# A hybrid attention kernel in one core: another order of its one list of steps

## The chip, the cores and the metric

One NeuronCore of a Trainium2 chip runs the kernel. The metric is the device time of one execution in microseconds. An engine of the core works through its own list of instructions in order and waits on semaphores for the others: PE (TensorE, the matmuls), ACT (ScalarE), DVE (VectorE), POOL (GpSimd), and SP, which here only issues transfers. An instruction that waits holds up everything behind it on its engine.

## What is computed

`x` holds 8 batches of 1024 tokens with 256 channels. The reference, cut to its core:

```
x = x + conv(gn(x))            # group norm; qkv = x @ w_qkv; q and k layer-normed per head;
                               # dots = k^T v per head; out = q @ dots / 1024
t = x + attn(ln(x))            # 8 heads of 32: softmax(q k^T / sqrt(32)) v, then @ w_agg + b_agg
t = t + ffn(ln(t))             # gates = 8 rounds of Sinkhorn; each of 8 experts takes its
                               # 128 best tokens per batch, multiplies by its 256 x 256 weights
```

## The kernel before

**Three things at a time.** While the softmax attention of batch b runs, the kernel does the linear attention and the projections of batch b+1 (the "front" steps) and the aggregation and layer norm of batch b-1 (the "store" steps). So the program is: a prologue with the front of batch 0 alone; eight stretches, one per batch attended, called batch 0 to batch 7 here; and a tail with the last store and the expert part. Batches 1 to 6 have all three kinds of work. Batch 0 has no store, batch 7 no front. Sinkhorn rounds are merged into batch 6, the selection of tokens into batch 7.

**Slots.** The attention of a batch is 64 units: scores of 128 keys by 256 queries by 4 heads on PE (L829, 4 matmuls), an exponential on ACT (L1123), the weighing by v on PE (L851). Eight units make a block, whose sum of probabilities DVE adds up (L1489, units 1 to 6 of a block). Two units are a slot, so that a batch has 32 slots, and a block ends every fourth slot: PE sums (`total`, L861), ACT copies the accumulator (L1113), DVE inverts it (L1474), POOL divides (L1156).

**The list of steps.** Everything else is a step. `order()` (L85) gives one hand-written list, in which `("rest", n)` leaves n slots empty; `spread()` (L70) deals the list to slots by the costs in `WORK`, and every engine walks the same plan. In a slot PE issues the scores of the next slot's two units, the first half of the steps, the weighing of its own two units, the second half. ACT has one exponential ahead of each half. DVE adds up between the halves. POOL has the steps only, and a division at the start of every slot with k % 4 = 1.

**The steps named below.** `xT` (c, h): 4 transposes of x on PE (L868), a copy on ACT (L1051), statistics on DVE. `agg` (t): aggregation on PE (L873), added and measured on DVE (L1255, L1249). `store_stats` and `head_stats`: chains of small POOL instructions for a reciprocal square root, each waiting for the one before. `store_rows` (t): the normalised rows on ACT (L1030). `z2T` and `gate`: transposes and gate logits of stored tokens. `gmean`, `gvar`, `xn`: the group norm of x. `qk0`, `v0`: queries, keys and values of the linear attention. `resid` (t): POOL adds the bias (L1192). `head_scale` (quarter): two instructions (L743); quarters 0 to 2 on POOL and 3 on DVE in batches 0 to 6. `qT` (c, h): transposes of scaled queries; h = 1 needs all four quarters. `dots`: 32 matmuls `shared<-rows,lo`. `lin` (t): its result times the queries. `zT`, `proj`, `v`, `norms`: the projections for the next attention. PE steps share two PSUM banks in turn: a step may start once the step two before it has been read.

## Time and profile before

| | |
|---|---|
| median of 3 runs | 1663.41 us (1662.82 to 1664.5) |
| profiled execution | 1661.75 us, span 1659.0 us |
| PE busy | 1390.6 us, 84% of the span |
| DVE busy | 1061.8 us, 64% |
| ACT busy | 872.8 us, 53% |
| POOL busy | 587.9 us, 35% |
| mean granted TensorE clock | 0.922 |

The prologue ends at 122.4 us, batch 0 runs to 279.6, batches 1 to 6 to 1315.5, batch 7 to 1454.6, and the rest is the tail. PE is the busiest engine in all of it but the tail. A granted clock of 1.00 is 2.4 GHz and 0.50 is 1.2 GHz.

### The profile page before, as it was taken

What the parts mean: (1) busy time and instruction counts of PE and PEld (TensorE: products, weight loads), DVE (VectorE), ACT (ScalarE), POOL (GpSimd) and SP (SyncE); (2) the same over time, 40 slices, a digit from 0 to 9 for tenths busy, and PEclk for the clock granted to TensorE, in tenths of its full rate; (3) what the DMA queues carried; (4) which work ended last, traced back from release to release, by engine and by line L of the source; (5) the groups of instructions that cost most, each with busy time, mean ns of one, the idle gap of its engine ahead of it and who ended that gap; (6) DMA issues with size and microseconds to landing.
All of it is one profiled execution on the core that took longest, in us unless ns stands there. A gap on an engine that the chain in (4) does not pass through costs nothing.

```text
span 1659.0 us, 27948 instructions
## 1 busy us (share of the span) xinstructions
PE 1390.6 (84%) x10311; PEld 923.7 (56%) x10311; DVE 1061.8 (64%) x2037; ACT 872.8 (53%) x1251; POOL 587.9 (35%) x1142
## 2 busy tenths in 40 slices
PE   5678899898989898989898999899988978976553
PEld 3445556556656656665656565656554655555432
DVE  3326776767675767585848585767678798645721
ACT  2336666666666566656665766566655555521100
POOL 1401520553034404341444134412442032455664
PEclk8889999999989999999999999999999988878777
DMA  2033004400440035003500260027000550243442
GB/s 70 26 91 75 1 26 106 125 13 26 92 138 13 27 77 153 13 27 72 158 14 6 68 182 14 1 58 197 14 2 1 117 166 11 83 148 112 128 144 71
DMA packets 66014, 119.07 MB, mean 72 GB/s; under 512 B 10321, under 2 KB 46162, under 8 KB 65874
## 3 DMA queue, kind: packets, MB, share of 16 engines
q1 hardware_dynamic: 56640, 92.04, 20.7%
q0 software_dynamic: 8192, 25.17, 4.9%
q8 instruction: 85, 1.39, 0.3%
q14 instruction: 55, 0.45, 0.1%
q10 hardware_dynamic: 1042, 0.01, 0.0%
HBM read 29.11 MB, written 33.55 MB: 38 GB/s over the span
## 4 chain that ended last, share of the span: by engine, by line
PE 51%; DVE 20%; issue 9%; POOL 8%; ACT 7%; SPq 2%; another core or an unknown queue 2%; DMA 0%; ACTq 0%; POOLq 0%; DVEq 0%
PE shared L873 29%; PE acc L851 8%; PE scores L829 8%; DVE prob_sum L1489 7%; PE shared L868 3%; DVE acc_sb L1474 3%; ACT probs L1123 2%; PE acc L861 2%; PE acc L848 1%; POOL out_dram L1228 1%; DVE bn L1249 1%; DVE best_i L1406 1%; POOL lo L743 1%; DVE work L1408 1%
## 5 line engine op out<-in xcount | busy, mean ns | idle before, releaser
L1123 ACT ACTIVATE probs<-scores 128x1024 f32<-128x1024 f32 x512 | 515.2, 1023 | 271.1 <-DVE prob_sum L1489 136.1
L1489 DVE TENSOR_TENSOR prob_sum<-prob_sum,probs 128x512 f32<-128x512 f32 x640 | 423.9, 722 | 0.0
L829 PE MATMUL scores<-query_stack,key_stack 96*128 96x256 f32 x2048 | 344.8, 308 | 44.7 <-ACT probs L1123 41.0
L829 PEld LDWEIGHTS scores<-query_stack,key_stack 96*128 96x128 f32 x2048 | 279.1, 196 | 123.2 <-ACT probs L1123 77.3
L851 PE MATMUL acc<-probs,v_all 128*32 128x256 f32 x4096 | 302.1, 402 | 0.4 <-issue 0.4
L1156 POOL TENSOR_TENSOR attn_T<-acc_sb 128x256 f32<-128x256 f32 x64 | 54.9, 858 | 546.8 <-DVE acc_sb L1474 537.0
L873 PE MATMUL shared<-w_sb,chan 128*128 128x512 f32 (+1 forms) x512 | 186.3, 500 | 5.0 <-DVE chan L1310 5.0
L851 PEld LDWEIGHTS acc<-probs,v_all 128*32 128x32 f32 x4096 | 117.2, 113 | 116.2 <-issue 43.8
L873 PE MATMUL shared<-chan,w1T 128*128 128x512 f32 x256 | 127.3, 622 | 8.8 <-DVE lo L1359 6.4
L1489 DVE TENSOR_TENSOR prob_sum<-probs 128x512 f32<-128x512 f32 x128 | 92.4, 762 | 56.6 <-PE acc L861 49.6
L873 PEld LDWEIGHTS shared<-w_sb,chan 128*128 128x128 f32 x512 | 91.1, 191 | 62.3 <-issue 56.0
L1474 DVE RECIPROCAL acc_sb<-acc_sb 128x256 f32<-128x256 f32 x64 | 111.6, 1744 | 21.9 <-ACT acc_sb L1113 21.1
L1359 DVE TENSOR_TENSOR lo<-shared,hi 128x512 fp32r<-128x512 f32 x64 | 44.1, 689 | 98.5 <-ACT hi L1076 98.5
L873 PE MATMUL shared<-lo,hi 128*128 128x256 f32 x256 | 77.3, 456 | 34.3 <-DVE chan L1444 17.4
L1325 DVE TENSOR_REDUCE ss<-v_all 128x16 f32<-128x512 f32 x64 | 43.6, 682 | 83.4 <-ACT v_all L1065 82.9
L1058 ACT ACTIVATE lo<-shared 128x512 f32<-128x512 f32 x64 | 38.2, 597 | 97.9 <-PE shared L873 97.9
L1106 ACT ACTIVATE hi<-shared 128x512 f32<-128x512 f32 x32 | 19.1, 597 | 134.2 <-remote 47.0
L873 PE MATMUL shared<-waggT,attn_T 128*128 128x256 f32 x256 | 74.2, 432 | 15.1 <-DVE resid L1255 14.8
L873 PEld LDWEIGHTS shared<-lo,hi 128*128 128x128 f32 x256 | 55.9, 229 | 48.0 <-DVE chan L1444 18.5
L1076 ACT ACTIVATE hi<-shared 128x512 fp32r<-128x512 f32 x64 | 38.2, 598 | 75.4 <-PE shared L873 75.4
L873 PEld LDWEIGHTS shared<-chan,w1T 128*128 128x128 f32 x256 | 45.3, 195 | 56.9 <-issue 42.8
L868 PE MATMUL shared<-ident,rows 128*128 128x128 f32 x256 | 47.2, 299 | 33.1 <-ACT rows L1030 23.2
(168 smaller groups left out, 2016.5 us busy)
## 6 DMA issues: line engine op xcount, KB each, us to landing
query_stack<-hi SPq DMA_DIRECT2D x128, 128.0 KB, 2.5
key_stack<-hi SPq DMA_DIRECT2D x128, 128.0 KB, 2.5
x_sb<-in_x_dram SPq DMA_DIRECT2D x8, 1024.0 KB, 5.6
key_stack<-lo SPq DMA_DIRECT2D x64, 128.0 KB, 2.5
query_stack<-lo SPq DMA_DIRECT2D x64, 128.0 KB, 2.4
out_dram<-resid SPq DMA_DIRECT2D x16, 512.0 KB
tokens_scratch<-resid SPq DMA_DIRECT2D x16, 512.0 KB
tokens_scratch<-rows SPq DMA_DIRECT2D x16, 512.0 KB, 3.3
```

Of the source, the lines that this page charges most:

```text
L829: last = pe.matmul(score_ps[u % 2][:, QB * r:QB * (r + 1)], key_stack[stack, HG * g + r, P * kt:P * (kt + 1)], query_stack[stack, HG * g + ...
L851: last = pe.matmul(acc[DH * r:DH * (r + 1), 0:QB], v_all[:, g, kt, DH * r:DH * (r + 1)], p[:, QB * r:QB * (r + 1)], start=kt == 0, stop=kt ...
L868: last = pe.transpose(ps[:, P * j:P * (j + 1)], m, ident[:, :])
L873: last = pe.matmul(out, stationary, moving, start=j == 0, stop=j == len(pairs) - 1)
L1058: read(act.activation(qk0[:, at[0], :], ps[:, :], ACT.Copy), seg, *st)
L1076: act.activation(hi[:, j, BANK * h:BANK * (h + 1)].bitcast(F32R), ps[:, :], ACT.Copy) \
L1123: act.activation(probs[:, u % PROBS, :], score_ps[u % 2][:, :], ACT.Exp, scale=DH ** -0.5) \
L1156: pool.tensor_tensor(attn_T[:, g, QB * qb:QB * (qb + 1)], acc_sb[:, 0:QB], acc_sb[:, QB:2 * QB], ALU.mult).then_inc(s["attn_ready"], 1)
L1325: dve.tensor_reduce(ss[:, t, :], squares[:, t % 2, :].rearrange("p (h d) -> p h d", d=DH), AX.X, ALU.add).then_inc(s["squares_summed"], 1)
L1359: read(dve.tensor_tensor(lo[:, j, part].bitcast(F32R), ps[:, :], hi[:, j, part], ALU.subtract), seg, *st)
L1474: dve.reciprocal(acc_sb[:, QB:2 * QB], acc_sb[:, QB:2 * QB]).then_inc(s["recip_ready"], 1)
L1489: dve.tensor_tensor(total[:, part], probs[:, (u - 1) % PROBS, part] if kt == 1 else total[:, part], probs[:, u % PROBS, part], ALU.add).th ...
```

## The change

Only the list in `order()` changes. Every step of before is still there once, in another place; `WORK`, `spread()` and the engines' code are the same. `rest` entries move, and shorter ones are used. Since the same plan also sets which PSUM bank a step gets, the turns of the two banks change with it.

```diff
-    steps = [("agg", 0), ("agg", 1), ("agg", 2), ("agg", 3), ("xT", 0, 0), ("xT", 0, 1), ("rest", 0.5),
+    steps = [("xT", 1, 0), ("xT", 0, 1), ("agg", 0), ("rest", 0.5), ("agg", 1), ("agg", 2), ("agg", 3),
...
-             ("head_scale", 1), ("head_stats", 1), ("rest", 1), ("resid", 6), ("resid", 7), ("sumv",), ("qT", 0, 0),
+             ("resid", 5), ("v0", 7), ("head_scale", 1), ("head_stats", 1), ("rest", 1), ("head_scale", 2),
```

Dealt to slots, batches 1 to 5 read so at the places of interest (a bar between the halves of a slot):

```
slot   before                                          after
0      agg0 agg1 agg2 | agg3 xT00 xT01                 xT10 xT01 | agg0 agg1
1      store_stats0 xT10 | agg4 xT11                   agg2 agg3 store_stats0 | xT11 xT00 agg4
2      agg5 x_stats agg6 gmean agg7 |                  agg5 x_stats agg6 store_rows0 gmean |
         store_rows0 gvar store_rows1 store_stats1       gvar agg7 store_rows1 store_stats1 store_rows2
3      z2T0 store_rows2 z2T1 | store_rows3 z2T2        z2T0 z2T1 | store_rows3
4      z2T3 | gate0                                    z2T2 z2T3 | xn0 gate0
5      xn0 | xn1
6                                                      qk00 gate1 | store_rows4
7      qk00 |                                          xn1 |
8      store_rows4 gate1 z2T4 v00 store_rows5 |        store_rows5 gate2 z2T4 store_rows6 |
         qk01 gate2 store_rows6 gate3                    gate3 v00 qk01 z2T5
12     resid4 v06 qk07 head_scale0 |                   resid4 v06 qk07 head_scale0 |
         resid5 v07 head_scale1                          resid5 v07 head_scale1 head_stats1
13     head_stats1 |
14     resid6 resid7 sumv | qT00 qT10 head_scale2      head_scale2 qT10 | qT00
15                                                     resid6 | sumv
16     head_scale3 |                                   head_scale3 | resid7
17     qT01 qT11 | dots                                qT11 | dots
19     lin0 | lin1                                     lin0 qT01 | lin1 lin2
20     lin2 lin3 front_stats0 | lin4 lin5 lin6         lin3 lin4 | front_stats0
21     lin7 |                                          lin5 lin6 | lin7
23     front_rows3 |                                   front_rows3 | zT10
24     zT00 zT10 | proj00                              zT00 front_rows4 front_rows5 | proj00 proj10
27-31  the same
```

First place: PE at the start of batch 1, slots 0 and 1. `waggT,attn_T` is agg (two matmuls each), `x_sb` is xT (four each). Before:

```order
L829 MATMUL scores<-query_stack,key_stack 128x256 x8
L873 MATMUL shared<-waggT,attn_T 128x256 x6
L861 MATMUL acc<-prob_sum,ones 32x256 x4
L851 MATMUL acc<-probs,v_all 32x256 x8
L873 MATMUL shared<-waggT,attn_T 128x256 x2
L868 MATMUL shared<-ident,x_sb 128x128 x8
L829 MATMUL scores<-query_stack,key_stack 128x256 x8
L868 MATMUL shared<-ident,x_sb 128x128 x4
L851 MATMUL acc<-probs,v_all 32x256 x8
L873 MATMUL shared<-waggT,attn_T 128x256 x2
L868 MATMUL shared<-ident,x_sb 128x128 x4
L829 MATMUL scores<-query_stack,key_stack 128x256 x8
```

And after:

```order
L829 MATMUL scores<-query_stack,key_stack 128x256 x8
L868 MATMUL shared<-ident,x_sb 128x128 x8
L861 MATMUL acc<-prob_sum,ones 32x256 x4
L851 MATMUL acc<-probs,v_all 32x256 x8
L873 MATMUL shared<-waggT,attn_T 128x256 x4
L829 MATMUL scores<-query_stack,key_stack 128x256 x8
L873 MATMUL shared<-waggT,attn_T 128x256 x4
L851 MATMUL acc<-probs,v_all 32x256 x8
L868 MATMUL shared<-ident,x_sb 128x128 x8
L873 MATMUL shared<-waggT,attn_T 128x256 x2
L829 MATMUL scores<-query_stack,key_stack 128x256 x8
```

Two xT now stand ahead of the first agg and the first `total`, and agg 0 to 3 fall on both sides of the scores of slot 1.

Second place: POOL in batch 1, from quarter 1 of head_scale (the first L743) to the start of the second head_stats chain (L336, then L338). L1156 is the division of a block. Before:

```order
L743 TENSOR_TENSOR lo<-lo,hr 128x512 x2
L1192 TENSOR_TENSOR resid<-lin_out,bias 128x256
L743 TENSOR_TENSOR lo<-lo,hr 128x512 x2
L1156 TENSOR_TENSOR attn_T<-acc_sb 128x256
L336 TENSOR_SCALAR hr<-ss 128x64
L338 TENSOR_TENSOR hh<-hr 128x64
```

After:

```order
L743 TENSOR_TENSOR lo<-lo,hr 128x512 x2
L1192 TENSOR_TENSOR resid<-lin_out,bias 128x256
L743 TENSOR_TENSOR lo<-lo,hr 128x512 x2
L336 TENSOR_SCALAR hr<-ss 128x64
L338 TENSOR_TENSOR hh<-hr 128x64
```

The division has left its place ahead of the chain. What follows the chain on POOL, from its third-last instruction on, before:

```order
L339 TENSOR_TENSOR hh<-hh,ss 128x64
L340 TENSOR_SCALAR hh<-hh 128x64
L341 TENSOR_TENSOR hr<-hr,hh 128x64
L1192 TENSOR_TENSOR resid<-lin_out,bias 128x256 x2
L743 TENSOR_TENSOR lo<-lo,hr 128x512 x2
L1156 TENSOR_TENSOR attn_T<-acc_sb 128x256
```

And after:

```order
L339 TENSOR_TENSOR hh<-hh,ss 128x64
L340 TENSOR_SCALAR hh<-hh 128x64
L341 TENSOR_TENSOR hr<-hr,hh 128x64
L1156 TENSOR_TENSOR attn_T<-acc_sb 128x256
L743 TENSOR_TENSOR lo<-lo,hr 128x512 x2
L1192 TENSOR_TENSOR resid<-lin_out,bias 128x256 x2
L1156 TENSOR_TENSOR attn_T<-acc_sb 128x256
```

The division comes behind the chain, and the two resid have gone from ahead of head_scale 2 to behind it.

Third place: PE in batch 1, slots 6 to 8. `w_sb,chan 128x512` is qk0, `w_sb,chan 128x256` is v0, `gate_w,hi` is gate, `ident,rows` is z2T. Before:

```order
L829 MATMUL scores<-query_stack,key_stack 128x256 x8
L873 MATMUL shared<-w_sb,chan 128x512 x2
L851 MATMUL acc<-probs,v_all 32x256 x4
L848 MATMUL acc<-probs,ones 32x256 x4
L851 MATMUL acc<-probs,v_all 32x256 x4
L829 MATMUL scores<-query_stack,key_stack 128x256 x8
L873 MATMUL shared<-gate_w,hi 128x8 x2
L868 MATMUL shared<-ident,rows 128x128 x2
L873 MATMUL shared<-w_sb,chan 128x256 x2
```

And after:

```order
L829 MATMUL scores<-query_stack,key_stack 128x256 x8
L873 MATMUL shared<-w_sb,chan 128x512 x2
L873 MATMUL shared<-gate_w,hi 128x8 x2
L851 MATMUL acc<-probs,v_all 32x256 x8
L829 MATMUL scores<-query_stack,key_stack 128x256 x8
L851 MATMUL acc<-probs,v_all 32x256 x4
L848 MATMUL acc<-probs,ones 32x256 x4
L851 MATMUL acc<-probs,v_all 32x256 x4
L829 MATMUL scores<-query_stack,key_stack 128x256 x8
L873 MATMUL shared<-gate_w,hi 128x8 x2
L868 MATMUL shared<-ident,rows 128x128 x2
```

qk0 0 and gate 1 come in slot 6, one slot and two slots earlier, and slot 7 has no PE step of its own.

## Rows read from the trace of the kernel before

**Rows 1.** Stretches of batch 3: length, busy us of engines, granted clock, DMA.

```profile
core 0: us, PE busy (x) PEld busy (x) DVE busy (x) ACT busy (x) POOL busy (x), PEclk, DMA share, GB/s
622.70:651.10 28.40, 24.97 (x212) 18.02 (x208) 20.48 (x52) 16.29 (x25) 9.40 (x31) 0.94 0.81 223
651.10:661.40 10.30, 9.10 (x86) 5.30 (x86) 9.80 (x17) 6.52 (x8) 9.31 (x13) 1.00 0.01 2
661.40:699.50 38.10, 35.75 (x245) 22.96 (x241) 17.46 (x34) 24.03 (x42) 15.08 (x29) 1.00 0.04 15
699.50:725.20 25.70, 21.38 (x190) 15.44 (x189) 19.06 (x24) 13.88 (x17) 14.10 (x19) 0.87 0.00 1
725.20:747.60 22.40, 19.21 (x207) 13.67 (x205) 20.24 (x45) 14.00 (x18) 8.21 (x24) 1.00 0.15 49
747.60:793.00 45.40, 43.95 (x308) 26.74 (x308) 27.97 (x42) 31.07 (x47) 3.40 (x12) 1.00 0.31 70
```

**Rows 2.** Chain that ended last, batches 3 and 4: start, us, what.

```profile
711.67 2.32 POOL resid L1192 x2
713.99 2.92 POOL lo L743 x2
...
882.01 2.32 POOL resid L1192 x2
```

**Rows 3.** Timeline of PE, batch 3: start, us, what, idle before and releaser.

```profile
637.31 3.64 PE L873 MATMUL shared<-waggT,attn_T 128*128 128x256 f32 x8 [2.23 <-DVE resid L1255]
...
663.84 0.41 PE L868 MATMUL shared<-ident,rows 128*128 128x128 f32 x2 [0.87 <-ACT rows L1030]
...
717.00 1.94 PE L868 MATMUL shared<-ident,lo 128*128 128x128 f32 x8 [3.66 <-POOL lo L743]
...
720.73 4.71 PE L873 MATMUL shared<-rows,lo 128*128 128x128 f32 x32
```

**Rows 4.** Granted clock in short stretches, columns as in rows 1.

```profile
637.30:640.70 3.40, 3.39 (x8) 2.55 (x9) 1.66 (x6) 1.24 (x2) 2.00 (x10) 0.50 0.91 231
717.00:722.60 5.60, 5.60 (x32) 4.00 (x33) 3.53 (x5) 2.60 (x4) 1.05 (x1) 0.50 0.00 1
```

**Rows 5.** Timeline of DVE, batch 3, slots 0 to 2.

```profile
631.51 1.74 DVE L1474 RECIPROCAL acc_sb<-acc_sb 128x256 f32<-128x256 f32 x1
...
634.44 2.48 DVE L1489 TENSOR_TENSOR prob_sum<-prob_sum,probs 128x512 f32<-128x512 f32 x4
636.84 0.41 DVE L1255 TENSOR_TENSOR resid<-shared,resid 128x256 f32<-128x256 f32 x1
```

**Rows 6.** Timeline of POOL, batch 3: store_stats 1, then head_stats 1.

```profile
650.97 0.44 POOL L1167 TENSOR_SCALAR ln_v<-mv 128x4 f32<-128x4 f32 x1 [0.20 <-POOL small L341]
...
653.67 2.77 POOL L340 TENSOR_SCALAR ln_h<-ln_h 128x4 f32<-128x4 f32 x1
...
656.98 3.99 POOL L338 TENSOR_TENSOR ln_h<-ln_r 128x4 f32<-128x4 f32 x1
...
662.17 0.23 POOL L1161 TENSOR_SCALAR ln_b<-ln_b 128x4 f32<-128x4 f32 x1
...
702.59 1.15 POOL L1156 TENSOR_TENSOR attn_T<-acc_sb 128x256 f32<-128x256 f32 x1 [4.18 <-DVE acc_sb L1474]
703.82 0.57 POOL L336 TENSOR_SCALAR hr<-ss 128x64 int32<-128x64 int32 x1
```

**Rows 7.** Timeline of DVE, batch 3, slots 4 to 7 and slot 12.

```profile
653.07 0.91 DVE L1310 TENSOR_SCALAR chan<-chan,small 128x512 f32<-128x512 f32 x2
653.89 2.49 DVE L1489 TENSOR_TENSOR prob_sum<-prob_sum,probs 128x512 f32<-128x512 f32 x4
...
699.49 0.67 DVE L1325 TENSOR_REDUCE ss<-v_all 128x16 f32<-128x512 f32 x1
```

**Rows 8.** Timeline of PE, batch 0: its dots, and a wait ahead of them.

```profile
198.00 1.22 PE L829 MATMUL scores<-query_stack,key_stack 96*128 96x256 f32 x4 [1.80 <-ACT probs L1123]
...
206.20 3.84 PE L873 MATMUL shared<-rows,lo 128*128 128x128 f32 x32
```

40 lines of the change are left out of this document (20 added, 20 removed).

## The prediction

> **What bounds the kernel now.** I read the stretches of one batch first, then the chain, then PE's timeline at its waits, and last the timeline of the engine that each wait names. Batches 1 to 6 are 1036 of the 1659 us and repeat themselves: the two resid of batches 3 and 4 start at 711.67 and 882.01, a period of 170.34 us [rows 2]. So I work on batch 3 and multiply by six. In its six stretches PE is busy 154.36 of 170.3 us, while DVE has 115.0 and ACT 105.8 [rows 1]. PE is the bound, and only two things can be had from it without taking work away: its idle time, 15.9 us, and the time in which its clock is at 0.50. Both sit at few places. The first stretch (slots 0 to 4) has 3.43 us idle, slots 5 to 7 have 1.20, slots 8 to 12 have 2.35, slots 13 to 17 have 4.32, slots 18 to 23 have 3.19, the rest 1.45 [rows 1]. The clock is at 0.50 for 3.4 us behind the wait of 2.23 us at 637.31, and for 5.6 us of busy PE behind the wait of 3.66 us at 717.00 [rows 3, 4]. Matmuls there take about twice their time: the 32 of dots take 4.71 us, of which only a part is slow, against 3.84 in batch 0 [rows 3, 8]. The two slow pieces cost 1.7 and 2.8 us (half of their length).
>
> The change takes no instruction away and adds none, so its worth is what it does to these waits. What I do below is to carry batch 3 through its new order by hand, with the durations of the rows.
>
> **Slots 13 to 17: head_stats, head_scale 2, qT, dots.** The chain of rows 2 and 6 reads: division 702.59, 1.15 us; the second head_stats chain from 703.82 to the first resid at 711.67, so 7.7 us; two resid, 2.32; head_scale 2, 2.92; then qT at 717.00, which waits for it 3.66 us [rows 2, 3, 6]. After: head_stats 1 is a step of slot 12. It needs the last sum of squares on DVE, which ends at 699.49 + 0.67 = 700.16 [rows 7], so the chain can start at about 700.3 and not at 703.8: 3.5 us earlier. The division follows the chain now, which adds and removes the same 1.15 us. The two resid have gone behind head_scale 2: 2.3 us more. Head_scale 2 ends at 716.9 - 3.5 - 2.3 = 711.1. PE is at its qT at 717.00 - 3.66 = 713.3, so the wait of 3.66 us goes, and with it what brought the clock down: 2.8 us. What is late next: sumv (0.95 us of PE) moves from slot 14 to slot 15, so that slot 14 has less to fill a wait for the exponentials, and the quarter on DVE (head_scale 3) has to be done by then. DVE finishes that quarter some 1.8 us after its sumv, at about 712.3, just ahead of 713.3. I put 0.5 to 1.5 us of new small waits there. So 6.5 - 0.5 = 6.0 at best, 2.2 (the wait alone, less 1.5) at worst; I take 4.8. The resid that are later wait for nobody until lin 0 in slot 19. qT (0, 1) moves behind lin 0, into slots 18 to 23 that have 3.19 us idle; if that cover were gone it would cost its half microsecond (eight transposes take 1.94 us at the low clock [rows 3]).
>
> **Slots 0 to 4: xT ahead of agg.** Agg 5 waits 2.23 us for DVE, which has first the inversion (1.74), then four additions (2.48), and only at 636.84 reads agg 4 [rows 3, 5]. After: PE gets to `total` behind 1.0 us of transposes instead of 2.75 us of agg, so ACT copies the accumulator and DVE inverts about 2.2 us earlier, ending near 631.0. Agg 0 to 3 are spread over two slots. In exchange, agg 4 is now read behind four additions and two statistics of xT (0.7 each), near 637.0, the same time as before; but PE does agg 5 before it has to wait, and the wait falls on agg 6 and is about 1 us. gmean then waits some 0.7 for DVE's mean, z2T 0 some 0.3. That leaves 2.0 us idle of 3.43, and no wait long enough to look like the one that was followed by the low clock. Best 1.4 + 1.7 = 3.1, worst 0 (the same idle time and the same clock); I take 2.2. ACT now has store_rows 0 in front of an exponential. Behind it wait the scores of slot 3; by my working the rows are free at 638.9, the exponential is out at 640.6, and PE asks for it at 641.4: 0.8 us of slack.
>
> **Slots 5 to 12: xn, gates, z2T.** These slots are short of DVE first: additions, inversion and two xn. z2T 4 waits 0.87 us for its rows [rows 3] and the gates right behind their z2T wait 0.3 to 0.5 each. After: xn 0 starts one slot earlier, gate 1 fills slot 6 where PE otherwise waits for exponentials, store_rows 4 comes a slot and a half ahead of z2T 4, and no gate directly follows its own z2T. I count 1.0 of the 1.20 us in slots 5 to 7 (gate 1 moves into them) and 1.5 of the 2.35 in slots 8 to 12. Bounds: 0 and 3.5 for both; taken 2.5.
>
> **Slots 18 to 31.** zT and proj change places with front_rows 4 and 5; DVE is busy 20.24 of 22.4 us in slots 18 to 23 and PE 43.95 of 45.4 behind them [rows 1], with the same work in both orders. I take 0, with -1.5 to 1.5 us.
>
> **The sum.** 4.8 + 2.2 + 2.5 + 0 = 9.5 us in a batch, 57 in six. Batch 0 has the same list without the store: its wait of 1.80 us with a low clock ahead of dots [rows 8] comes from the same late quarter; I take 3.5 (1.8 to 5.5). The prologue has one qT less ahead of its dots and starts qk0 behind one xn: 1.5 (0 to 3). Batch 7 and the tail: 0 (-2 to 2). Together 62 us. The profiled execution took 1661.75 us, so 1599.75; the median of the runs is 1.66 above that execution, so 1601.4 us.
>
> **Rivals.** First, store_rows in front of the exponentials. ACT reaches store_rows 4 in slot 6 at about 655.0 by my working, and needs the store_stats 1 chain. That chain took from 650.97 to 662.4, 11.4 us for 17 small instructions, because one of them lasted 2.77 and one 3.99 us; both start beside an xn of DVE and end only when a row of additions behind it ends [rows 6, 7]. It would now start at 647.8, and with the same two stalls end at 659.2: exponentials and then PE 3.5 to 4.2 us late. That eats the 4.7 us of slots 0 to 12 but for one: 5.8 a batch, 35 + 5 = 40 us, 1623. For it: both stalls come in nearly every batch. Against it: xn 0 is now followed by an inversion and not by additions, and xn 1 comes when the chain should be over.
>
> On this the Trainium skill, "SBUF — State Buffer", on who interferes with whom, says that VectorE and GpSimd lock a port pair for a whole instruction and that the loser is blocked until that one ends. By that rule alone a stall is one DVE instruction (about 0.7 us) and not 2.77 or 3.99; the chain would take some 6.4 us and end at 654.3, ahead of ACT, and 1601 would stand. The trace disagrees: the stall of 2.77 us spans all four additions from 653.89 to 656.38.
>
> Second, the low clock at dots stays, since the short waits of slots 14 to 16 do what the long one did. Then 2.8 us a batch are lost: 6.7 a batch, 40 + 5 = 45, 1618.
>
> Third, nothing is gained: DVE, with 20.24 of 22.4 us in slots 18 to 23 [rows 1], takes back what PE had won, so that each batch ends when it did. For it: exponentials there wait for additions. Against it: DVE's own waits in those slots end with PE's results, which come earlier too. 1663.
>
> Fourth, slower: POOL is shut out longer. Every POOL chain now runs earlier, beside xn 0 and denser additions. If store_stats 1 had its two stalls twice (6.8 us more, 18.2 in all), it would end at 666, and ACT would stand 11 us at store_rows 4. Less the 4.7 gained and the 4.8 at dots, that is 1.5 us a batch lost; with one stall of 4 us in head_stats 1, whose slack is 2.2, it is 3.3: 20 us, 1683. It decides from a store_stats 1 chain of about 17 us on. Against it: while ACT stands still, DVE soon has nothing to add and leaves POOL alone.
>
> **How the numbers follow.** The forecast has 0.59, the first rival 0.22, the second 0.07, the third 0.03, the fourth 0.09. Under 0.2% (3.3 us) a measurement of this kernel can't tell a change from none. Faster is the first three cases, 0.88; same is 0.03; slower is 0.09. The forecast's own range comes from its bounds: 6.5 to 12 us a batch and 0 to 10 for the rest give 1581 to 1624. The range given reaches from 1584 to 1640, a first rival in which slots 0 to 12 give nothing or a little less.
>
> **What would show it.** A period between the same instructions of two batches of about 161 us instead of 170.3. No wait on POOL's head_scale ahead of qT, head_scale 2 done ahead of PE's qT, dots in 3.8 us. Agg 5 without a wait, one of about 1 us at agg 6, clock 1.00 behind it. Store_rows 4 on ACT with no wait for POOL. It is wrong if ACT waits for POOL in slot 2 or slot 6 for more than 1 us, if the clock is at 0.50 in dots, or if the idle time of PE in a batch is still above 12 us.

## The result, and the profile after

The changed kernel took 1573.56 us (median of 4 runs, 1566.26 to 1576.86), the kernel before 1663.12 us beside it (4 runs, 1656.24 to 1664.5): a ratio of 0.9452 with a 95% interval from 0.9434 to 0.9469, so 89.6 us less. The forecast was 1601.4 us in a range from 1584 to 1640: the right sign, and too small by a third.

| | before | after |
|---|---|---|
| profiled execution, span | 1661.75, 1659.0 us | 1566.26, 1564.0 us |
| PE busy | 1390.6 us, 84% | 1364.3 us, 87% |
| POOL busy | 587.9 us | 564.2 us |
| mean granted clock | 0.922 | 0.934 |
| prologue and batch 0 | 280.4 us | 280.8 us |
| batches 1 to 6 | 1036.5 us | 950.0 us |
| batch 7 | 137.7 us | 130.9 us |
| tail | 204.4 us | 202.3 us |

The last four rows are worked out from the starts of the exponentials (512 in the program, 2 in a slot), and so is every gain of a stage below: the time from the first exponential of one slot to that of another, as the mean of batches 1 to 6. Batches 1 to 6 gave 86.5 us, 14.4 each, where the forecast had 57, 9.5 each. Prologue and batch 0 gave nothing, where it had 5. Batch 7 and the tail gave 8.9, where it had 0.

Batch 3 after the change in its six stretches, cut at the same slots as [rows 1]: length, busy us of each engine with its instructions, granted clock, DMA.

```profile
core 0: us, PE busy (x) PEld busy (x) DVE busy (x) ACT busy (x) POOL busy (x), PEclk, DMA share, GB/s
592.60:617.20 24.60, 23.50 (x212) 17.14 (x209) 19.93 (x52) 16.06 (x25) 9.46 (x33) 1.00 0.84 222
617.20:626.30 9.10, 9.10 (x91) 5.83 (x90) 8.41 (x15) 6.27 (x8) 5.98 (x15) 1.00 0.29 98
626.30:661.60 35.30, 34.80 (x239) 22.27 (x236) 18.75 (x36) 24.11 (x41) 13.30 (x24) 1.00 0.05 16
661.60:681.00 19.40, 18.26 (x186) 13.44 (x185) 18.91 (x22) 13.04 (x16) 14.25 (x20) 1.00 0.01 2
681.00:703.00 22.00, 19.22 (x212) 13.92 (x210) 21.19 (x48) 14.49 (x18) 8.46 (x23) 1.00 0.17 49
703.00:747.30 44.30, 43.82 (x310) 26.84 (x308) 28.11 (x42) 31.40 (x47) 3.78 (x12) 1.00 0.32 72
sum 154.70, PE 148.70 PEld 99.44 DVE 115.31 ACT 105.37 POOL 55.23; mean PE 24.78 PEld 16.57 DVE 19.22 ACT 17.56 POOL 9.21
```

The batch has gone from 170.3 to 154.7 us. PE's idle time fell from 15.9 to 154.70 - 148.70 = 6.0 us, and its busy time by 5.7 us with the same instructions, the clock being 1.00 now in all six stretches. Batch 3 is a good one in this: the clock is at 0.50 for 3.4 us in slots 18 to 23 of batches 2 and 4 and for 6.8 us in those of batch 5, and batches 1 to 5 last 154.2, 155.6, 154.7, 155.7 and 156.8 us. DVE's and ACT's busy times are as they were. The second to fourth stretches have next to no idle PE left (0.00, 0.50, 1.14 us); what remains stands in the fifth (2.78), where DVE is busy 21.19 of 22.00 us. POOL lost 23.7 us in the program, above all the two stalls of 2.77 and 3.99 us [rows 6]. Both stood in five of the six batches, the shorter one alone in batch 2; after the change there is none.

PE at the places of [rows 3], batch 3 after: start, us, what, idle before and releaser.

```profile
603.03 1.13 PE L873 MATMUL shared<-waggT,attn_T 128*128 128x256 f32 x4 [0.25 <-ACT chan L1051]
...
606.48 1.13 PE L873 MATMUL shared<-waggT,attn_T 128*128 128x256 f32 x4 [0.50 <-DVE resid L1255]
...
609.20 0.35 PE L873 MATMUL shared<-small,gn_mean 128*128 128x2 f32 x2 [0.20 <-DVE small L1301]
...
628.40 0.42 PE L868 MATMUL shared<-ident,rows 128*128 128x128 f32 x2
...
675.90 0.60 PE L868 MATMUL shared<-ident,lo 128*128 128x128 f32 x4
...
677.43 3.84 PE L873 MATMUL shared<-rows,lo 128*128 128x128 f32 x32
```

The wait of 2.23 us ahead of agg 5 has become three of 0.25, 0.50 and 0.20 us, and the clock stays up. Z2T 4 doesn't wait, qT doesn't wait, and dots take 3.84 us, the value of full clock [rows 8].

POOL after, batch 3: store_stats 1, then the start of head_stats 1, head_scale 2, and the first two resid behind it.

```profile
616.03 0.23 POOL L1167 TENSOR_SCALAR ln_v<-mv 128x4 f32<-128x4 f32 x1 [0.19 <-POOL small L341]
...
619.83 0.80 POOL L338 TENSOR_TENSOR ln_h<-ln_r 128x4 f32<-128x4 f32 x1
...
622.80 0.23 POOL L1161 TENSOR_SCALAR ln_b<-ln_b 128x4 f32<-128x4 f32 x1
...
663.68 0.24 POOL L336 TENSOR_SCALAR hr<-ss 128x64 int32<-128x64 int32 x1 [1.46 <-DVE ss L1331]
...
672.66 2.50 POOL L743 TENSOR_TENSOR lo<-lo,hr 128x512 f32<-128x512 f32 x2
675.13 2.31 POOL L1192 TENSOR_TENSOR resid<-lin_out,bias 128x256 f32<-128x256 f32 x2
```

The store_stats 1 chain took 7.0 us (616.03 to 623.03), against 11.4 [rows 6]; its longest instruction is 0.80 us. Head_scale 2 ends at 675.16, 0.74 us before PE gets to its qT at 675.90.

Each kernel that follows takes some slots of batches 1 to 6 from the list of before and the rest from the changed one; the planner's outcome is cut by slots (0 to 4, 5 to 12, 13 to 18, 19 to 31), so the letters below say for four pieces which is old (o) and which is new (n). A step that this would leave out is put in by hand (xn 0 at the head of slot 5, head_stats 1 at the head of slot 13, qT (0, 1) at the head of slot 17); one that would stand twice is kept at its first place. So the late qT (0, 1), in slot 19 behind lin 0, stands in none of the first four kernels. The arithmetic is the same in all of them. All but the first two rows of the table are one execution each, and are compared by their stages, which come out of the profile and do not depend on the tail. Three chips took part, and the kernel before took 1663.12 us on the first (the pair above), 1640.08 us (median of 7, 1638.46 to 1646.17) on the second (p1 to s0) and 1670.19 us on the third (u1 to u3). The gains are against the one profile of before, from the first chip.

How far such a gain can be trusted is seen in slots 0 to 4, which eight of the runs leave as they were and which gain -0.25 to 1.22 us there. In these runs and in the kernel before they last 26.9 to 27.1 us in a batch where the granted clock stays at 1.00, 28.1 to 28.4 where it is at 0.50 for 3.4 us, 28.9 with 6.8 us and 30.2 to 30.3 with 10.2 us, with the same instructions.

| run | us | slots 0–4 | 5–12 | 13–17 | 18–31 | a batch |
|---|---|---|---|---|---|---|
| changed kernel | 1573.56 | 3.78 | 4.07 | 5.83 | 0.74 | 14.41 |
| the same again | 1555.47 | 3.78 | 4.07 | 5.82 | 0.63 | 14.29 |
| p1, new 0–4 | 1626.12 | 3.79 | -1.05 | 0.42 | -0.29 | 2.87 |
| p2, new 5–12 | 1615.79 | -0.12 | 3.17 | 2.09 | -0.53 | 4.61 |
| p3, new 13–18 | 1619.4 | -0.11 | -0.31 | 2.83 | 0.02 | 2.43 |
| p4, new 19–31 | 1631.75 | 0.49 | 0.01 | -0.44 | 0.64 | 0.70 |
| q1, p3 + chain early | 1626.3 | -0.25 | -0.33 | 4.16 | -0.75 | 2.83 |
| q2, p2 - chain early | 1622.96 | 0.27 | 2.70 | -0.36 | 0.30 | 2.91 |
| r2, q1 + late qT | 1605.26 | 0.53 | 0.01 | 6.05 | -0.79 | 5.79 |
| q3, changed, old 19–31 | 1581.37 | 3.79 | 4.06 | 2.32 | -0.57 | 9.59 |
| r1, changed, qT early | 1569.39 | 3.78 | 4.07 | 3.13 | 0.90 | 11.90 |
| r3, q3 + late qT | 1572.28 | 3.77 | 4.07 | 5.83 | -2.00 | 11.68 |
| q4, changed, old batch 0 | 1551.71 | 3.79 | 4.06 | 5.83 | 0.67 | 14.34 |
| u1, new 5–7 | 1649.55 | 0.66 | 1.43 | 0.45 | -0.71 | 1.83 |
| u2, new 8–12 | 1628.74 | 1.22 | 2.29 | 3.06 | -0.25 | 6.32 |
| u3, changed, sumv early | 1579.24 | 3.79 | 4.06 | 5.70 | 0.54 | 14.09 |

### The profile page after: what moved, and what is told of

Read it like the earlier page. It is cut to its first block, busy times and chain, and to the rows that moved or that the text cites. A ratio compares the mean times of both kernels' runs of the same rounds, so it can differ in the third digit from the quotient of the medians.

```text
span 1564.0 us, 27948 instructions
## 1 busy us (share of the span) xinstructions
PE 1364.3 (87%) x10311; PEld 912.5 (58%) x10311; DVE 1062.3 (68%) x2037; ACT 869.9 (56%) x1251; POOL 564.2 (36%) x1142
## 3 DMA queue, kind: packets, MB, share of 16 engines
q1 hardware_dynamic: 56640, 92.04, 22.1%
## 4 chain that ended last, share of the span: by engine, by line
PE 55%; DVE 22%; issue 7%; ACT 5%; POOL 4%; SPq 2%; another core or an unknown queue 2%; DMA 1%; DVEq 0%; ACTq 0%; POOLq 0%
PE shared L873 29%; PE scores L829 10%; PE acc L851 9%; DVE prob_sum L1489 9%; PE shared L868 3%; ACT probs L1123 3%; DVE acc_sb L1474 2%; PE acc L861 2%; PE acc L848 1%; DVE bn L1249 1%; DVE best_i L1406 1%; DVE work L1408 1%; DVE best L1404 1%; SPq L465 1%
## 5 line engine op out<-in xcount | busy, mean ns | idle before, releaser
L851 PE MATMUL acc<-probs,v_all 128*32 128x256 f32 x4096 | 296.2, 397 | 0.0
L1156 POOL TENSOR_TENSOR attn_T<-acc_sb 128x256 f32<-128x256 f32 x64 | 55.5, 866 | 522.7 <-DVE acc_sb L1474 515.5
L1489 DVE TENSOR_TENSOR prob_sum<-probs 128x512 f32<-128x512 f32 x128 | 97.0, 799 | 59.3 <-PE acc L861 55.3
L873 PE MATMUL shared<-chan,w1T 128*128 128x512 f32 x256 | 123.0, 610 | 3.5 <-DVE lo L1359 2.0
L873 PE MATMUL shared<-lo,hi 128*128 128x256 f32 x256 | 83.9, 487 | 29.5 <-issue 8.6
L873 PEld LDWEIGHTS shared<-lo,hi 128*128 128x128 f32 x256 | 60.0, 246 | 45.2 <-issue 10.9
L873 PE MATMUL shared<-waggT,attn_T 128*128 128x256 f32 x256 | 67.2, 396 | 6.6 <-DVE resid L1255 5.0
L873 PE MATMUL shared<-w1T,chan 128*128 128x256 f32 x256 | 62.3, 386 | 3.2 <-DVE lo L1359 2.7
```

Source lines behind the costliest of these rows:

```text
L851: last = pe.matmul(acc[DH * r:DH * (r + 1), 0:QB], v_all[:, g, kt, DH * r:DH * (r + 1)], p[:, QB * r:QB * (r + 1)], start=kt == 0, stop=kt ...
L873: last = pe.matmul(out, stationary, moving, start=j == 0, stop=j == len(pairs) - 1)
L1156: pool.tensor_tensor(attn_T[:, g, QB * qb:QB * (qb + 1)], acc_sb[:, 0:QB], acc_sb[:, QB:2 * QB], ALU.mult).then_inc(s["attn_ready"], 1)
L1489: dve.tensor_tensor(total[:, part], probs[:, (u - 1) % PROBS, part] if kt == 1 else total[:, part], probs[:, u % PROBS, part], ALU.add).th ...
```

## Experiments: each piece of the list alone

**p1_start**

```
return mixed(old, new, "nooo") if full else old
```

> The kernel before, with only slots 0 to 4 of batches 1 to 6 in the new order (xn 0 stays in slot 5). Parts add up: the period of a batch falls from 170.3 by 3.5 to 4.5 us (the whole change was 3.8 us ahead at slot 5), the wait ahead of agg 5 is gone and the clock behind it is 1.00; the run is 24 us faster (21 to 27). Rival, parts depend on each other: what is won at slot 4 is given back at the next wait for POOL or ACT (z2T 4 in slot 8), and the period falls by under 2 us.

One thing in that text is wrong: xn 0 stands in slot 4 here, its place in the new order. The batch gained 2.87, under the 3.5 to 4.5 expected and over the rival's 2. Slots 0 to 4 gave 3.79 us, as much as in the changed kernel, so what they win needs nothing of the rest. But 1.05 was given back in slots 5 to 12, and the timeline of PE shows it beside the old wait of z2T 4 [rows 3]:

```profile
646.98 0.75 PE L924 MATMUL scores<-query_stack,key_stack 96*128 96x256 f32 x4 [1.54 <-ACT probs L1218]
...
654.44 0.41 PE L963 MATMUL shared<-ident,rows 128*128 128x128 f32 x2 [0.86 <-ACT rows L1125]
```

PE waits for an exponential, which waits 2.26 us for DVE: with the old slots behind it, both xn, a gate, the inversion and ten additions stand in one row on DVE. The same row does to POOL what the fourth rival feared. POOL, then DVE of this kernel, in the same 7 us:

```profile
643.84 0.34 POOL L427 TENSOR_TENSOR ln_h<-ln_h,ln_v 128x4 f32<-128x4 f32 x1
644.27 6.39 POOL L428 TENSOR_SCALAR ln_h<-ln_h 128x4 f32<-128x4 f32 x1
```

```profile
642.02 1.74 DVE L1569 RECIPROCAL acc_sb<-acc_sb 128x256 f32<-128x256 f32 x1
643.68 0.90 DVE L1405 TENSOR_SCALAR chan<-chan,small 128x512 f32<-128x512 f32 x2
644.50 6.10 DVE L1584 TENSOR_TENSOR prob_sum<-prob_sum,probs 128x512 f32<-128x512 f32 x10
```

An instruction that otherwise takes 0.2 us lasts 6.39. It begins beside xn 1 and ends when the tenth addition does, and it is so in all of batches 1 to 6 (6.38 or 6.39 each).

**p2_middle**

```
return mixed(old, new, "onoo") if full else old
```

> The kernel before, with only slots 5 to 12 of batches 1 to 6 in the new order (xn 0 at the head of slot 5; head_stats 1 in slot 12 comes with it). Parts add up: between slot 5 and slot 13 the whole change won 3.9 us, and that much is won here; head_stats 1 one slot earlier on POOL gives 3.5 us more at qT, so the period falls by 7 to 7.5 us. Rival, the gates only move the same waits: under 2 us between slots 5 and 13, and the period falls by 3.5 to 5.5 us.

The batch gained 4.61, in the rival's range and not the 7 expected. It has two effects: 3.17 in its own slots, and 2.09 in slots 13 to 17, since head_stats 1 has gone to slot 12 with them. Before qT PE still waits (the view names no releaser; POOL's head_scale 2 ends at 702.14), and a short low clock follows:

```profile
702.24 1.29 PE L963 MATMUL shared<-ident,lo 128*128 128x128 f32 x8 [1.90 <-issue]
...
705.32 4.32 PE L968 MATMUL shared<-rows,lo 128*128 128x128 f32 x32
```

Against [rows 3] the wait went from 3.66 to 1.90, and dots from 4.71 to 4.32: less of them falls into the low clock.

**p3_dots**

```
return mixed(old, new, "oono") if full else old
```

> The kernel before, with only slots 13 to 18 of batches 1 to 6 in the new order: head_stats 1 stays at the head of slot 13, behind the division; the two resid come behind head_scale 2, sumv in slot 15, qT (0, 1) behind dots (it waits in slot 19). If the resid alone matter: POOL is 2.3 us earlier, the wait of 3.66 us shrinks to 1.3 us, the clock stays at 1.00, and the period falls by 4 to 5 us. Rival, the chain of head_stats is what decides: the wait stays above 3 us, the clock at dots is 0.50, and the period falls by under 2 us.

One thing in that text is wrong: qT (0, 1) doesn't stand behind dots here. It was put in at the head of slot 17, ahead of qT (1, 1) and dots, and so in q1.

```profile
710.67 1.06 PE L963 MATMUL shared<-ident,lo 128*128 128x128 f32 x8 [0.89 <-POOL lo L838]
...
714.12 3.84 PE L968 MATMUL shared<-rows,lo 128*128 128x128 f32 x32 [1.38 <-ACT hi L1166]
```

Putting the two resid behind head_scale 2 alone takes 2.8 us from the wait and brings the clock back, but a new wait of 1.38 us stands ahead of dots: for ACT, which has to read what qT (0, 1) left in the PSUM buffer that dots take next. The gain is 2.83, not the 4.8 forecast for all of these slots, and 2.43 in the batch, where 4 to 5 were expected.

**p4_end**

```
return mixed(old, new, "ooon") if full else old
```

> The kernel before, with only slots 19 to 31 of batches 1 to 6 in the new order (qT (0, 1) stays in slot 17): zT 1 in slot 23, proj 1 in slot 24, front_rows 4 and 5 ahead of proj 0. By my prediction 0 (-1.5 to 1.5 us a batch). By the traces of the whole change 1.7 us a batch were won in these slots, 10 us in the run, if that comes from their own order. Rival: it comes from DVE, which had less waiting when the slots ahead were changed; then the period is within 0.5 us of 170.3.

Slots 18 to 31 gave 0.64, the whole batch 0.70, between the 1.7 and the rival's 0.5 of the text. The four pieces alone add up to 2.87 + 4.61 + 2.43 + 0.70 = 10.6 us, and the whole change is worth 14.4. Of the 3.8 us between them 2.5 is the late qT (0, 1), which no piece has (r1 below), and 1.3 is what the pieces do for each other: slots 5 to 12 gave -1.05 in p1 and 3.17 in p2, and 4.07 in the changed kernel.

## Experiments: what dots need

**q1_dots_and_chain** (p3, and head_stats 1 from slot 13 to 12)

```
out[13].remove(("head_stats", 1)); out[12].append(("head_stats", 1))
```

> The kernel before, with slots 13 to 18 of batches 1 to 6 in the new order and head_stats 1 at the end of slot 12 as well; the gates and everything else as before. Theory, both moves on POOL are needed together at dots: slots 0 to 13 as before, no PE wait over 1 us ahead of qT, clock 1.00 at dots, and slot 18 is reached 6 us earlier counted from slot 13 (the resid alone gave 3.4 to 3.9 there, the chain alone 1.2 to 2.7); period down by 5.5 to 6.5 us, clock phase aside. Rival, ACT and DVE bound slots 14 to 16 anyway: not over 4 us, no more than the resid alone.

**q2_middle_no_chain** (p2, and head_stats 1 back from slot 12 to 13)

```
out[12].remove(("head_stats", 1)); out[13].insert(0, ("head_stats", 1))
```

> The kernel before, with slots 5 to 12 of batches 1 to 6 in the new order, but head_stats 1 back at the head of slot 13. What the gates, z2T, xn and store_rows 4 are worth by themselves: 4.0 to 4.4 us between slot 5 and slot 13 as with head_stats 1 (2.8, 4.2 and 4.2 in batches 1, 3 and 5), and then the old wait of 3.66 us and the low clock at dots, so nothing more by slot 18. Rival, head_stats 1 had a share in it: 1 us less by slot 13.

**r2_all_of_dots** (q1, and qT (0, 1) from slot 17 to 19, behind lin 0)

```
out[17].remove(("qT", 0, 1)); out[19].insert(1, ("qT", 0, 1))
```

> The kernel before, with all that the change does around dots in batches 1 to 6 and nothing else: slots 13 to 18 new, head_stats 1 at the end of slot 12, qT (0, 1) behind lin 0 in slot 19. If the three parts add up (resid behind head_scale 2; chain earlier, together 5 us at slot 18 in the last study; qT late, 2.4): 6 to 7 us won from slot 13 to slot 18, as in the whole change, and a period 5.5 to 6.5 us shorter. Rival: without the other slots' changes ACT comes late to slot 17 and under 5 us are won.

In slots 13 to 17 the resid alone gave 2.83 (p3), with the chain 4.16 (q1), and with the late qT 6.05 (r2). The early chain alone gave 2.09 (p2), and p2 without it -0.36 there (q2). Dots in q1, then in r2:

```profile
708.81 3.84 PE L972 MATMUL shared<-rows,lo 128*128 128x128 f32 x32 [1.66 <-ACT hi L1170]
```

```profile
701.78 3.84 PE L974 MATMUL shared<-rows,lo 128*128 128x128 f32 x32
```

So three moves make up the 5.8 us, and the last of them, the one that the prediction called a matter of its own half microsecond, is worth 1.9 here. It takes away a wait for ACT, not PE work. The clock is at 1.00 in these slots in all three of p3, q1 and r2, so that no fall of it is in these differences. R2's batch gained the 5.5 to 6.5 us expected. Q1's gained 2.83 where 5.5 to 6.5 were expected, and the middle without the chain gave 2.70 (q2) where 4.0 to 4.4 were.

**q3_new_but_end** (the changed kernel with slots 19 to 31 of before)

```
return mixed(old, new, "nnno") if full else new
```

> The changed kernel, with slots 19 to 31 of batches 1 to 6 in the old order (qT (0, 1) back in slot 17). If the 1.7 us that slots 18 to 31 won in the whole change come from their own order, the period rises by 1.5 to 2 us from 154.7 to 156.8, and the run is 9 to 12 us slower. If they come from what is ahead of them, the period stays within 0.5 us. That the new order is worse there by itself (by up to 0.9 us in batch 5 with the rest old) would show as a shorter period.

**r1_new_qT_first** (the changed kernel, qT (0, 1) from slot 19 to 17)

```
new[19].remove(("qT", 0, 1)); new[17].insert(0, ("qT", 0, 1))
```

> The changed kernel, with qT (0, 1) back at the head of slot 17 in batches 1 to 6, ahead of qT (1, 1) and dots. Theory: dots then takes its PSUM bank from qT (0, 1), which ACT has to read first; with the transposes themselves (0.5 us) that is a wait of about 1.4 us ahead of dots, slot 18 is reached 2.4 us later, and the period is 2 to 2.5 us longer. Rival: slot 18 is 0.5 us later, the time of the transposes, and slot 19 gets it back.

**r3_new_but_end_qT_late** (q3, and qT (0, 1) from slot 17 to 19)

```
out[17].remove(("qT", 0, 1)); out[19].insert(1, ("qT", 0, 1))
```

> The changed kernel, with slots 19 to 31 of batches 1 to 6 in the old order, except that qT (0, 1) stays behind lin 0 in slot 19. The same kernel with qT (0, 1) ahead of dots had a period 4.6 to 5.3 us longer than the changed one. If half of that is qT, the period is now 2 to 3 us longer than the changed one (156.7 to 159), and the rest is the new order of lin, zT, proj and front_rows. Rival, all of it is qT: the period is within 0.7 us of the changed one.

Q3 lost 4.8 us a batch, 3.5 of it in slots 13 to 17, which it shares with the changed kernel but for qT (0, 1). R1 moves that step alone and loses 2.7 there and 2.5 in the batch. R3 puts it back into q3 and has 5.83 again. For q3 the text had 1.5 to 2 us, for r1 and r3 2 to 3, so q3 alone missed. Q3 loses more than r1 in slots 13 to 17 because the clock falls there in four of its six batches and in one of r1's: with such a fall of 3.4 us they last 22.9 us in both, without it 21.3, against 18.9 in the changed kernel. So 2.4 us is the late qT itself. Dots of q3 show the same wait as p3:

```profile
690.16 3.84 PE L968 MATMUL shared<-rows,lo 128*128 128x128 f32 x32 [1.91 <-ACT hi L1166]
```

What r3 still lacks, 14.41 - 11.68 = 2.7 us, is the new order of slots 19 to 31. It shows at two places, slots 20 to 22 and slot 26. Here r3, then the changed kernel, in the columns of the stretches above:

```profile
696.50:710.00 13.50, 10.62 (x112) 7.72 (x114) 12.64 (x32) 7.71 (x10) 6.17 (x20) 0.99 0.25 79
724.90:733.80 8.90, 7.62 (x42) 3.85 (x41) 5.62 (x10) 6.16 (x11) 0.00 (x0) 1.00 0.00 0
```

```profile
688.40:700.90 12.50, 10.03 (x108) 7.26 (x111) 11.96 (x31) 7.85 (x10) 6.62 (x20) 1.00 0.12 25
716.80:722.30 5.50, 5.06 (x37) 2.94 (x36) 4.18 (x7) 4.47 (x8) 0.00 (x0) 1.00 0.01 3
```

Slot 26 shrinks from 8.9 to 5.5 us. Part of that is work that the new order has elsewhere (5 matmuls, 3 DVE and 3 ACT instructions fewer), and part is idle PE, 1.28 against 0.44. The length of one slot alone therefore isn't a gain; the stage's is. The same order gives 0.64 in p4 and 2.7 here, and the profiles show where the difference lies. Mean us of batches 1 to 6, and the time at a granted clock of 0.50:

| | slots 18–23 | of it at 0.50 | slots 24–31 |
|---|---|---|---|
| before | 23.66 | 2.3 | 47.37 |
| p4, the new order alone | 24.74 | 5.0 | 45.65 |
| r3 | 25.44 | 4.8 | 47.59 |
| changed kernel | 24.70 | 3.4 | 45.59 |

In slots 24 to 31 the new order is worth 1.7 us in p4 and 2.0 against r3, so it needs nothing of the rest. The two comparisons differ in slots 18 to 23, where the clock is low for longer: a batch of p4 with no fall there takes 21.52 us, of before 21.63, and one of before with 3.4 us of low clock 22.95. P4, batch 3, slots 18 to 23 and 24 to 31:

```profile
720.20:744.00 23.80, 21.35 (x206) 15.06 (x205) 19.47 (x45) 14.82 (x19) 10.46 (x33) 0.86 0.15 46
744.00:788.60 44.60, 44.11 (x310) 27.13 (x310) 28.41 (x42) 31.03 (x46) 1.46 (x2) 1.00 0.31 71
```

Why the clock falls in some batches and not in others no run shows.

## Experiments: the middle slots, and what is left

**u1_slots_5_to_7** (old list, new slots 5 to 7)

```
return old[:5] + [[("xn", 0)] + new[5]] + new[6:8] + old[8:]      # no step twice
```

> The kernel before, with only slots 5 to 7 of batches 1 to 6 in the new order: qk0 0, gate 1 and store_rows 4 in slot 6, xn 1 in slot 7 (xn 0 at the head of slot 5), the rest as before. Slots 5 to 12 as a whole won 2.7 us with their new order in the kernel before, without the earlier head_stats 1. Theory, what matters is that store_rows 4 and gate 1 are far behind their producers: 1.5 to 2.5 us of it come here, and the wait of PE ahead of z2T 4 is gone. Rival: store_rows 4 in slot 6 makes ACT wait for POOL, and slots 5 to 12 win under 0.5 us.

**u2_slots_8_to_12** (old list, new slots 8 to 12)

```
out = old[:8] + new[8:13] + old[13:]                              # no step twice
out[8][:0] = [("gate", 1), ("store_rows", 4)]; out[12].append(("head_stats", 1))
```

> The kernel before, with only slots 8 to 12 of batches 1 to 6 in the new order (store_rows 4 and gate 1 at the head of slot 8, head_stats 1 at the end of slot 12), the rest as before. Theory as for slots 5 to 7: what is left for the gates behind their z2T is 0.5 to 1.5 us in slots 5 to 12, and the earlier head_stats 1 gives 2 us more by slot 18. Rival, the order inside slots 8 to 12 is the source: 2 to 3 us in slots 5 to 12.

Of the 2.70 us that the middle is worth without the chain (q2), u1 has 1.43 and u2 2.29 in its slots (together more than 2.70, so the two overlap). Most of it is the order inside slots 8 to 12, where I had expected 0.5 to 1.5: my theory fell, and the rival held. U1's 1.43 is just under its 1.5. Z2T 4 in u1 and then in u2, where it waited 0.87 before [rows 3]:

```profile
656.58 0.38 PE L969 MATMUL shared<-ident,rows 128*128 128x128 f32 x2
```

```profile
650.87 0.41 PE L969 MATMUL shared<-ident,rows 128*128 128x128 f32 x2 [0.42 <-ACT rows L1131]
```

U1 removes the wait and wins less; u2 keeps half of it and wins more. So the wait that the prediction looked at isn't the large one. Slot 9 is: in all kernels with the new slots 8 to 12 it lasts 6.64 us with 0.05 of idle PE, in the others 8.94 with 1.13. U2 has 3.06 in slots 13 to 17 as well, where p2 with the same chain has 2.09: its slot 17 lasts 6.10 against 7.35. The difference is the clock, which falls there in all six batches of p2 and in one of u2. Slots 13 to 17 of batch 3, p2 and then u2:

```profile
687.50:710.10 22.60, 20.00 (x187) 14.07 (x187) 20.02 (x24) 12.81 (x15) 13.77 (x19) 0.92 0.01 1
685.40:706.80 21.40, 18.56 (x187) 13.38 (x187) 20.08 (x24) 12.81 (x15) 13.77 (x19) 1.00 0.01 2
```

**u3_new_sumv_early** (the changed kernel, sumv from slot 15 to the end of slot 14)

```
new[15].remove(("sumv",)); new[14].append(("sumv",))
```

> The changed kernel, with sumv back at the end of slot 14 in batches 1 to 6, where PE waits 0.16 and 0.78 us for exponentials. If PE's work is what bounds slots 13 to 17, sumv (0.95 us) fills the wait and a batch is 0.5 to 0.9 us shorter, the kernel 3 to 5 us faster. Rival, DVE bounds slots 14 to 22 (it is idle 0.0 to 0.5 us in each): nothing is won, within 0.3 us a batch.

The period is 158.65 us, against 158.46 and 158.33 in the two profiles of the changed kernel. PE's wait for an exponential in slot 14 goes from 0.78 us in the changed kernel

```profile
669.29 0.74 PE L829 MATMUL scores<-query_stack,key_stack 96*128 96x256 f32 x4 [0.78 <-ACT probs L1123]
```

to 0.18, and the batch doesn't gain by it. In these stretches DVE is busy 18.91 of 19.40 and 21.19 of 22.00 us: it is the bound there now, and filling PE's idle time is worth nothing. In u3 DVE is idle for 0.03 us in slots 13 to 17 of batch 3.

**q4_new_batch0_old** (the changed kernel, the list of before in batch 0)

```
return old if seg.has("attend") and not seg.has("store") else new
```

> The changed kernel, with batch 0 in the old order. Batch 0 took 159.0 us in the new order and 156.8 in the old, in five traces of the old one always 156.7 to 156.9. So batch 0 takes 156.8 again, the kernel is 2.2 us faster than the changed one, and batches 1 to 6 are as they were. Rival: the prologue's new order hands batch 0 over in another state and is the cause; then batch 0 still takes about 159.

**s0_after_again** (the changed kernel once more, timed in turn with the kernel before)

```
(no edit)
```

> The changed kernel once more, timed in turn with the kernel before on this chip. In seven traces of other kernels, batch 7 with unchanged code took 125.8 to 132.5 us and the tail 189.1 to 194.6, against 137.7 and 204.4 in the trace of before: 16 us or more of the difference of 95 us between the two first traces would then be no effect of the order. Theory: what the order gives is 86 us in batches 1 to 6 and about 2 in the prologue and batch 0, so the ratio is 0.946 to 0.949. Rival: batch 7 really gains 7 us by its order; the ratio is 0.942 or lower.

S0 took 1555.47 us (4 runs, 1555.03 to 1555.96) against 1640.08: 84.6 us, a ratio of 0.9478 (0.9455 to 0.9502), as expected. Both kernels are faster on this chip, and the ratio agrees with the first pair's: the two intervals overlap. Its six batches are those of the changed kernel, and so are q4's.

Batch 0 takes 158.4 to 160.8 us in the six kernels with the new order (mean 159.7) and 156.7 to 159.0 in the eleven with the old one (mean 157.3). The old one has two lengths: 156.7 to 156.9 in eight of them, and 158.7 to 159.0 in q1, u1 and q4, which are the three with the shortest prologue (120.8 to 121.6 us, the others 122.7 to 125.1). Q4 has the new prologue and the old batch 0. So the text for q4 missed: batch 0 took 158.7 us and not 156.8. But its rival is no cause either, since q1 and u1 have the same length with the old prologue. What the three share is the clock in slots 0 to 4: 7.9 to 8.2 us at 0.50 and 22.2 to 22.4 us, where the eight have 2.7 to 5.9 and 20.3 to 20.5. The new batch 0 gains nothing and more likely loses a little, while the new prologue is shorter by 1.2 in the mean (122.2 of seven, 123.4 of ten).

No version beats the changed kernel: q4's 1551.71 is one run, and its lead over s0 is in batch 7 and the prologue, not in a batch that the change orders.

The first pair's 8.9 us of batch 7 and tail aren't the change's either. P4 differs from the kernel before in nothing there, and takes 26 us less. Before, then p4, batch 7 and tail, in the same columns:

```profile
1317.00:1454.60 137.60, 115.77 (x1003) 77.03 (x996) 114.08 (x228) 74.40 (x91) 45.72 (x64) 0.85 0.31 92
1454.60:1659.00 204.40, 115.84 (x488) 88.87 (x486) 87.77 (x240) 26.41 (x48) 118.56 (x146) 0.76 0.39 122
```

```profile
1314.00:1440.40 126.40, 108.62 (x998) 72.65 (x991) 114.79 (x228) 74.52 (x92) 48.62 (x64) 0.88 0.35 100
1440.40:1630.10 189.70, 115.92 (x493) 88.89 (x491) 87.54 (x240) 26.35 (x48) 118.50 (x146) 0.79 0.43 132
```

In the tail the busy times agree within 0.3 us and the length differs by 14.7: it is waiting. What waited there in the kernel before (all of the tail; us, times, longest):

```profile
ACT hi L1106 <- remote: 45.8, 6, 10.0
DVE chan L1444 <- remote: 19.3, 2, 13.6
```

These are waits of the steps that follow the gathers of tokens; the profile names nothing on this core that ended them. On the second chip the tail is 189.1 to 194.6 us and no run has such a wait, on the third it is 208.3 to 209.8, and the waits are back. In batch 7 PE itself is 7.2 us busier in the kernel before, at a lower clock.

## Why the prediction was too small, point by point

**What bounds the kernel** held. PE's idle time and its low clock were what could be had, at the places named, and no instruction had to go: 9.9 us of idle time and 5.7 us of busy time in batch 3, of the 15.9 and 4.5 that were seen. The price of the low clock was a little high: half of 3.4 us is 1.7, but slots 0 to 4 with such a piece last only 1.3 us longer than without it (28.3 and 27.0).

**Slots 0 to 4** (2.2 taken, 0 to 3.1): 3.8 measured, alone and together. The step that failed is the sentence that 2.0 us of idle time would be left: about 1 us at agg 6, 0.7 at gmean, 0.3 at z2T 0. The rows show 0.50, 0.20 and, unforeseen, 0.25, and 1.10 us in all of these slots, so that 2.3 us of idle time went and not 1.4. I had put agg 4's read behind four additions and two statistics, near 637.0, the time it had before. In the profile PE gets to `total` earlier, so DVE has the inversion earlier (598.78, 6.2 us into the batch, where it was 8.8), and the row behind it ends earlier too:

```profile
598.78 1.74 DVE L1474 RECIPROCAL acc_sb<-acc_sb 128x256 f32<-128x256 f32 x1
...
602.44 2.46 DVE L1489 TENSOR_TENSOR prob_sum<-prob_sum,probs 128x512 f32<-128x512 f32 x4
604.82 1.28 DVE L1286 BATCH_NORM_STATS2 bn_x<-chan 128x6 f32<-128x512 f32 x2
606.02 0.74 DVE L1255 TENSOR_TENSOR resid<-shared,resid 128x256 f32<-128x256 f32 x2
```

Agg's read comes 13.4 us into the batch, where it was 14.1 [rows 5].

**Slots 5 to 12** (2.5 taken, 0 to 3.5): 4.1, above the bound. 2.7 of it is the order itself (q2), and the earlier chain adds nothing here: four batches of p2 take 46.0 us, as q2's do. The other 1.4 comes when these slots are entered in another state. They take 44.6 us (44.9 in batch 3) behind the new slots 0 to 4, with xn 0 in slot 4, and 44.6 also in batches 3 and 5 of p2, with xn 0 in slot 5, behind slots 0 to 4 of 30.25 us. P1 has xn 0 in slot 4 and lost 1.05 with the old order. What it is in that state no run isolates. The step that failed is the bound, which was PE's idle time in those slots (3.55 us [rows 1]). That went but for 0.5; the rest is PE's busy time, 44.85 us before and 43.90 after in batch 3 with the same steps, at a clock of 1.00 in both, and why it shrank is open. Inside it, 1.5 for slots 8 to 12 was the mis-sized term (u2: 2.29). It looked at z2T 4 and the gates and not at slot 9, whose idle time of 1.13 us went.

**Slots 13 to 17** (4.8 taken, 2.2 to 6.0): 5.8. The mechanism held as written: a wait of 3.66 us and the low clock behind it, removed by an earlier chain and later resid, worth 4.2 of it (q1). The chain started 2.4 us earlier in its slots and not 3.5, because the last sum of squares moved too, and that was enough by 0.74 us. The discount of 0.5 to 1.5 for new small waits was a guess. What the prediction had at no more than half a microsecond, qT (0, 1), carried 1.9 (r2 over q1) to 2.7 (the changed kernel over r1): it would have been the next wait, 1.4 to 1.9 us for ACT ahead of dots, had it not been moved. The forecast had the right total for this stage and missed one of its three causes. The price of that one was the step that failed: a step moved was priced by its own transposes and not by the buffer turn that it gives up.

**Slots 18 to 31** (0, -1.5 to 1.5): 0.74, in the bound, but by two things that offset each other. The new order gave 1.8 us in slots 24 to 31, where the prediction put it at nothing because the work is the same, and 1.0 was lost in slots 18 to 23, which took qT (0, 1) and have 1.1 us more of low clock in the mean. Against r3, which has all the rest, the order is worth 2.7.

**Batch 0 and the prologue** (3.5 and 1.5): -0.4 in the pair. Over all profiles the prologue gave 1.2, close to its term, and batch 0 cost 2.4 where 3.5 were to be had. The gain at dots was there: slots 13 to 17 of batch 0 take 24.6 us before and 22.1 in the changed kernel (20.2 in s0). What failed is that the term had no price for the rest of the batch. Slots 0 to 4, before and then after, took back more:

```profile
126.00:146.20 20.20, 15.62 (x158) 11.05 (x158) 14.09 (x30) 12.40 (x15) 3.86 (x13) 0.93 0.55 137
124.20:150.90 26.70, 21.33 (x162) 13.21 (x162) 13.46 (x29) 13.15 (x16) 2.51 (x13) 0.79 0.43 107
```

Some of these 6.5 us come back in slots 5 to 12 (44.1 to 41.8), and 2.0 more are lost in slots 18 to 23. PE is busy longer with nearly the same instructions, at a granted clock of 0.79 against 0.93; what made the clock fall there is open.

**Batch 7 and the tail** (0, -2 to 2): 8.9 in the first pair, from nothing in the change. The range was a guess; unchanged code there has spread over 30 us.

**The rivals.** The first, store_rows in front of the exponentials with POOL's stalls, didn't come about. ACT, batch 3, store_rows 0 and 4:

```profile
608.49 0.60 ACT L1030 ACTIVATE rows<-resid,ln_b,ln_r 128x256 f32<-128x256 f32 x1 [2.79 <-POOLq L1170]
...
623.94 0.60 ACT L1030 ACTIVATE rows<-resid,ln_b,ln_r 128x256 f32<-128x256 f32 x1
```

Store_rows 4 waits for nothing, since the chain was not shut out; store_rows 0 waits 2.79 us for POOL, over the 1 us that was to prove the forecast wrong, and yet costs PE at most a part of the 1.10 us that it is idle in all of slots 0 to 4. That sign was badly chosen; a wait on ACT counts when PE's next exponential is late. The reason given against the rival, that xn 0 is now followed by an inversion and not by additions, agrees with the profile and with p1: there xn 1 is followed by ten additions and POOL stands 6.39 us. By the Trainium skill, "SBUF — State Buffer", on who interferes with whom, the port pair is held for a whole instruction and the loser is blocked until that one ends. As in the trace before, p1 shows more: POOL blocked over ten. The second rival (low clock stays) is refuted by dots of 3.84 us, the third by the period, the fourth by the chain of 7.0.

**The sum.** 86.5 - 57 = 29.5 us more in the six batches; 0.4 lost instead of 5 gained in prologue and batch 0, 5.4 less; 8.9 more in batch 7 and tail. That is 33.0, and the span was 95.0 us shorter where 62 was forecast. The upper ends of the three terms, 3.1, 3.5 and 6.0, would have been 12.6 a batch, of 14.4. I took values below them although no row showed the waits that I subtracted. The range has the same fault. With the 1.5 of slots 18 to 31 the upper ends make 14.1 a batch, 84.6 in six, and with the 10 for the rest 94.6 us, so 1568.8 us for the kernel. The prediction went to 12 a batch and to 1584 with no reason given, and 1573.56 lies between the two. 8.9 us of the 95.0 came from nothing in the change; without them the kernel would have taken about 1582 us, still under 1584.
